# Expert rows transposed in 32x32 blocks by VectorE and moved through memory, expert weights resident in SBUF, a new order of steps

## What is computed

```python
x  = hidden                                  # (4, 512, 256) f32
xn = layernorm(x)
# attention part (RWKV): k, v, r are projections of xn mixed with xn one step earlier
m_new = max(mx + w, k); m_out = max(mx, k + time_first)
e1, e2 = exp(mx - m_out), exp(k + time_first - m_out)
out = (e1*num + e2*v) / (e1*den + e2)
e1, e2 = exp(mx + w - m_new), exp(k - m_new)
num, den = e1*num + e2*v, e1*den + e2        # scanned over 512 positions
s = (sigmoid(r) * out) @ Wo.T
# mixture of experts: 16 experts, each token takes 4
h = silu(xn @ w_gate[e]) * (xn @ w_up[e])    # 256 -> 256
ffn += coeff[:, None] * (h @ w_down[e])      # 256 -> 256
result = x + s * silu(ffn)
```

## Time and profile before

| what | value |
|---|---|
| median of 3 runs | 346.5 us (344.99 to 347.97) |
| the profiled execution | 347.63 us |
| its span, first to last instruction | 345.7 us |
| mean granted clock of TensorE | 0.965 |
| loop over units (39) | from about 83 us to 305 us |

### The profile page before, as it was taken

The page is one execution under the profiler, slowest core; times in us unless marked ns, Lnnn a source line. Parts: engine busy times, 40 slices in busy tenths (PEclk is TensorE's granted clock), DMA queues, the critical chain, the costliest instruction groups (busy, mean ns, idle before and its releaser), DMA issues.

```text
span 345.7 us, 4753 instructions
## 1 busy us (share of the span) xinstructions
PE 299.8 (87%) x1413; PEld 236.0 (68%) x1414; DVE 253.4 (73%) x498; ACT 153.3 (44%) x236; POOL 225.5 (65%) x223
## 2 busy tenths in 40 slices
PE   0798999797999999999999999999999999799000
PEld 0334444345888888888888888888888888588000
DVE  2879899859589597795995959959687010189992
ACT  1891864224644635628247273463652323172220
POOL 3500399948767777777777777777777724257363
PEclk9999999998999999999999999999999999999755
DMA  7894000043656557656475666656465698587132
GB/s 236 279 392 191 1 0 1 8 131 89 177 175 207 159 172 232 215 146 205 144 254 141 211 171 203 208 195 186 153 211 171 216 361 302 194 280 238 43 121 91
DMA packets 31723, 61.46 MB, mean 178 GB/s; under 512 B 4620, under 2 KB 22029, under 8 KB 31568
## 3 DMA queue, kind: packets, MB, share of 16 engines
q10 hardware_dynamic: 6848, 21.26, 19.8%
q1 hardware_dynamic: 17360, 21.24, 18.1%
q0 software_dynamic: 7488, 18.63, 17.3%
HBM read 48.52 MB, written 14.42 MB: 182 GB/s over the span
## 4 chain that ended last, share of the span: by engine, by line
PE 68%; DVE 12%; POOL 9%; DMA 6%; issue 3%; POOLq 0%; ACT 0%; ACTq 0%; DVEq 0%
PE ps L545 60%; POOL ohB L334 8%; DVE arena L983 5%; PE ps L650 5%; DMA rows<-y_rows 3%; PE ps L555 2%; DMA wrou<-wrouT_in 1%; DVE arena L998 1%; POOL arena L352 1%; DMA arena<-xn_rows,tok_idx 1%; DVE arena L758 1%; DVE rows L733 1%; DMA y_rows<-arena,e_idx 1%; DVE vT L767 1%; DVE rows L814 0%
## 5 line engine op out<-in xcount | busy, mean ns | idle before, releaser
L545 PE MATMUL ps<-arena,rows 128*128 128x256 f32 x624 | 142.8, 383 | 2.4 <-issue 2.4
L545 PEld LDWEIGHTS ps<-arena,rows 128*128 128x128 f32 x624 | 116.8, 192 | 17.2 <-issue 3.0
L352 POOL DMA_INDIRECT arena<-xn_rows,tok_idx x78 | 83.5, 1070 | 27.6 <-issue 21.0
L359 POOL DMA_INDIRECT y_rows<-arena,dst_idx x66 | 72.8, 1103 | 22.3 <-issue 19.8
L911 DVE TENSOR_TENSOR arena<-arena,ps 128x512 f32<-128x512 f32 x39 | 26.3, 675 | 65.7 <-PE ps L545 34.1
L545 PE MATMUL ps<-wdn,arena 128*128 x312 | 73.7, 380 | 0.0
L545 PEld LDWEIGHTS ps<-wdn,arena 128*128 128x128 f32 x312 | 59.3, 190 | 8.2 <-issue 0.3
L498 ACT COPY arena<-ps 128x512 f32<-128x512 f32 x39 | 22.8, 584 | 83.4 <-PE ps L545 83.4
L334 POOL TENSOR_SCALAR ohB<-late 128x128 f16<-128x128 f32 x24 | 30.7, 1291 | 24.9 <-DVE late L819 24.9
L545 PE MATMUL ps<-arena 128*128 128x512 f32 x96 | 45.5, 607 | 0.4 <-DVE arena L758 0.4
L493 ACT ACTIVATE arena<-ps 128x512 f32<-128x512 f32 x39 | 23.5, 602 | 27.5 <-PE ps L545 27.3
(11 more groups left out here) (140 smaller groups left out, 332.3 us busy)
## 6 DMA issues: line engine op xcount, KB each, us to landing
rows<-wgu_in ACTq DMA_DIRECT2D x39, 512.0 KB, 3.8
rows<-y_rows SPq DMA_DIRECT2D x3, 2048.0 KB, 11.1
wdn<-wd_in SPq DMA_DIRECT2D x1, 4096.0 KB, 14.4
rT<-x_in SPq DMA_DIRECT2D x4, 512.0 KB, 6.0
xn_rows<-rT SPq DMA_DIRECT2D x4, 512.0 KB, 3.6
kT<-x_in SPq DMA_DIRECT2D x8, 256.0 KB, 3.3
rows<-y_rows SPq DMA_DIRECT2D x8, 256.0 KB, 5.0
out<-arena SPq DMA_DIRECT2D x8, 256.0 KB, 2.1
```

What stands on the lines that cost most here:

```text
L352: pool.indirect_dma_start(out=xg[i % XG][:, j, :], out_offset=None, in_=xn_rows, in_offset=bass.IndirectOffsetOnAxis(ap=tok_idx[:, 2 * i + ...
L359: pool.indirect_dma_start(out=y_rows, in_=ysb[:, par, j, :], in_offset=None, out_offset=bass.IndirectOffsetOnAxis(ap=idx[:, n + j:n + j + ...
L545: ins = nc.tensor.matmul(dst, lhsT(c), rhs(c), start=(c == 0), stop=(c == C - 1))
```

## The change

Six things change together.

1. From unit 4 on (`EARLY`) PE no longer transposes x. DVE transposes the gathered rows in blocks of 32x32 (`quad_x`, one instruction on 128x512), three units ahead of `hidden` (`AHEAD`). SP stores the result to DRAM (256 KB, `store_x`) and loads it back with four DMAs of 64 KB that move the blocks to their partitions (`load_xT`). Units 0 to 3 are transposed by PE as before.
2. The gate and up weights of all 16 experts (8 MB) are loaded into SBUF once, in place of 512 KB for each unit. For each unit ACT copies its expert's weights (128x1024) to one of two small buffers (`copy_expert`).
3. PE's step is now `down(i - 2)` and then `gate_up(i)`.
4. DVE's parts 1 and 2 of the scan write two differences where they wrote four and a maximum (3 instructions fewer in a piece). ACT makes the four tensors from them with two Relu instructions (scale 1 and -1) ahead of the exp.
5. LAG goes from 6 to 8, and `gather(i)` waits for `quad_x(i - 4)`.
6. SP's stream now holds the stores and loads of x for every unit, and the loads of slots 0 to 2 of `y_rows` stand behind them all. The down weights are loaded in two halves.

The core of the diff:

```diff
-            def load_expert(i):
+            def copy_expert(i):
                 wait(act, up_psum, i - 1)
                 expert = act.value_load(unit_expert[0:1, i:i + 1], min_val=0, max_val=E - 1)
-                act.dma_start(wgu[:, i % 2].rearrange("p c n -> p (c n)"),
-                              wgu_in[bass.ds(expert, 1)].rearrange("a p n -> p (a n)")).then_inc(wgu_loaded[i % 2], 16)
+                nc.scalar.copy(wgu[i % 2].rearrange("p c n -> p (c n)"),
+                               wgu_all[:, bass.ds(expert, 1), :].rearrange("p a n -> p (a n)")).then_inc(wgu_copied, 1)
...
-            def step(i, blocks=None):
-                evac_x(i)
-                if i > 0:
-                    if i <= NEED and (i - 1) % HALF == 1:
-                        piece = (i - 1) // HALF
-                        act.wait_ge(args_ready, piece + 1)
-                        nc.scalar.activation(args, args, ACT.Exp).then_inc(exps_ready, 1)
-                    silu(i - 1, (i - 1) % 2)
-                    if i + 1 < NP:
-                        next_expert(i + 1, blocks)
+            def step(i):
+                if i < EARLY:
+                    evac_x(i)
                 if i > 1:
                     evac_y(i - 2, i % 2, 32 * ((i - 2) // 2))
+                if i < NEED and i % HALF == 1:
+                    act.wait_ge(args_ready, i // HALF + 1)
+                    for part, sign in ((args[:, 2:4, :], -1.0), (args[:, 0:2, :], 1.0)):
+                        nc.scalar.activation(part, gaps, ACT.Relu, scale=sign).then_inc(act_step, 1)
+                    act.wait_ge(act_step, 2 * (i // HALF + 1))
+                    nc.scalar.activation(args, args, ACT.Exp, scale=-1.0).then_inc(exps_ready, 1)
+                silu(i, i % 2)
+                if i + 2 < NP:
+                    copy_expert(i + 2)
...
+            def store_x(i):
+                sp.wait_ge(xq_ready, i - EARLY + 1)
+                sp.dma_start(xq_rows[i], xq[:, i % 2, :]).then_inc(xq_stored[i % 2], 16)
+
+            def load_xT(i, par, stored):
+                sp.wait_ge(up_psum, i - 1)
+                sp.wait_ge(xq_stored[par], stored)
+                for q in range(NQ):
+                    sp.dma_start(xTg[q * QUAD:(q + 1) * QUAD, par, :].rearrange("p (i n) -> p i n", i=NQ),
+                                 xq_rows[bass.ds(i, 1), :, q * P:(q + 1) * P].rearrange("a (i p) n -> p (a i) n", p=QUAD)
+                                 ).then_inc(xT_in[par], 16)
+
+            def step(i):
+                if i >= EARLY:
+                    store_x(i)
+                if i > EARLY:
+                    load_xT(i - 1, (i - 1) % 2, 16 * ((i - 1 - EARLY) // 2 + 1))
...
             def step(i):
-                transpose_x(i)
-                if i > 0:
-                    gate_up(i - 1, (i - 1) % 2, 16 * ((i - 1) // 2 + 1))
+                if i < EARLY:
+                    transpose_x(i)
...
                 if i > 1:
                     down(i - 2, i % 2, expert_of(i - 2))
+                gate_up(i, i % 2)
...
-                    V.scalar_tensor_tensor(out=e_keep, in0=m_old, scalar=w, in1=m_new, op0=ALU.add, op1=ALU.subtract)
-                    V.tensor_tensor(e_new, k, m_new, ALU.subtract)
-                    link(V.scalar_tensor_tensor(out=ta, in0=k, scalar=first, in1=m_old, op0=ALU.add, op1=ALU.max))
+                    V.scalar_tensor_tensor(out=gaps[:, 0], in0=m_old, scalar=w, in1=k, op0=ALU.add, op1=ALU.subtract)
                 elif part == 2:
-                    V.tensor_tensor(o_keep, m_old, ta, ALU.subtract)
-                    V.scalar_tensor_tensor(out=o_new, in0=k, scalar=first, in1=ta, op0=ALU.add,
+                    V.scalar_tensor_tensor(out=gaps[:, 1], in0=k, scalar=first, in1=m_old, op0=ALU.add,
                                            op1=ALU.subtract).then_inc(args_ready, 1)
...
+            def quad_x(i):
+                dve.wait_ge(xg_in[i % XG], 32 * (i // XG + 1))
+                if i >= EARLY + 2:
+                    dve.wait_ge(xq_stored[i % 2], 16 * ((i - EARLY) // 2))
+                V.transpose(xq[:, i % 2, :].rearrange("p (q m c) -> p m q c", q=NQ, c=QUAD),
+                            xg[i % XG].rearrange("p t (c q r) -> p (t c) q r", c=C, q=NQ)).then_inc(xq_ready, 1)
...
             def step(i):
+                next_quad_x(i + AHEAD)
                 piece, u = divmod(i, HALF)
```

More of the change, by code:

```diff
@@ L920, in wkv @@
                 m_old, m_new = mrun[:, 0:SEQ], mrun[:, 1:SEQ + 1]
[L921 removed]
+                e_new, o_keep, e_keep, o_new = (args[:, a, :] for a in range(4))
                 H = SEQ // 2
@@ L970, in step @@
                     wkv(piece // C, piece % C, part)
-            for i in range(FIRST - 1):
+            for i in range(FIRST):
+                if i == FIRST - AHEAD:
+                    blocks, low = units_used(dve)
                 step(i)
-            blocks, low = units_used(dve)
-            optional(dve, blocks, lambda i: step(i - 1))
-            hidden(low + LAG - 1, (FIRST - 1) % 2)
+            optional(dve, blocks, step)
             def weighted(n, k):
```

141 lines of the change are left out of this document (85 added, 56 removed).

## The result

| what | before | changed |
|---|---|---|
| median | 347.24 us (4 runs, 344.99 to 348.06) | 379.62 us (4 runs, 377.16 to 380.02) |
| ratio, 95% interval | 1 | 1.0944 (1.0899 to 1.0988) |
| the profiled execution, its span | 347.63, 345.7 us | 379.92, 378.2 us |
| mean granted clock | 0.965 | 0.936 |

The changed kernel is 9.4% slower, 13.6 us above the forecast of 366 and inside its range.

The account below looks back on a forecast made before the run. DVE with ACT was to become the bound in place of PE: 22.30 - 1.99 + 1.83 + 3.28 = 25.4 us a piece. With start, last units and tail the span is 365, + 1.93 - 1.13 gives 366 us; range 356 to 382.

Parts of the forecast that it names:

- transposes at the scan's price: Rival: each block transpose on DVE takes 1.22 us in place of 0.61, + 15 us: 381; chance 0.20 together with x late.
- units 29 to 38: End of the loop, PE alone setting the pace at last: last hidden at about 319 us, where it was 302.10, +17.
- What bounds the kernel: In the loop: PE needs 22.48 us a piece of four units; DVE with ACT, a closed loop, runs at 22.30.
- Transposes on DVE: In a piece: four block transposes at 0.61 us, one falling into DVE's wait, three lengthening the loop by 1.83 us.
- ACT in a piece: From args to hidden: two Relus and the exp's exposed table load add 3.28 us, between 2.0 and 3.5.
- The loop: DVE and ACT become the bound: 25.4 us a piece against PE's 20.7; seven such distances make 178 us, where it was 156.1.
- The start: First units: ACT's copies of experts' weights put hidden(1) at 98.4 in place of 95.85 us, +2.6, between 0 and +4.
- SP and the tail: After the loop: loads of slots 0 to 2 go out behind load_xT(38), at about 311 us, in a row; span 365.
- PE sets the pace: Rival: DVE and ACT need under 20.7 us a piece, all 15.4 us are kept: 334 us; faster had chance 0.04.
- x comes too late: Rival: in the last units PE waits for load_xT, 0.6 to some 5 us a unit: 374, up to 400.
- Transposes dearer or x late: The two rivals of dearer DVE transposes and late x taken together: 372 to 390 us, chance 0.20.
- The clock fell: Rival: PE's clock falls in its new pauses; 4 us at the lower level cost 2 us a piece, sum unchanged; chance 0.03.

Follow-up runs that it names:

- e4: Kernel before with only the two Relus on ACT in place of three DVE instructions: 357.59 us, ratio 1.0289.
- e5: Kernel before with one block transpose of 128x512 on DVE in each of 33 steps, of other data into an unread scratch: 360.22 us, ratio 1.0388.
- e1: Changed kernel with an exp of one column ahead of ACT's wait for the args, to load the exp's table there: 373.73 us, ratio 1.0697.
- e6: Changed kernel with all x transposed by PE, LAG 6, no block transposes and no stores and loads of x: 390.02 us, ratio 1.1225.
- e9: e8 with x of units 1 to 3 transposed by PE and copied by ACT one step earlier: 347.24 us, ratio 1.0041.
- e7: Changed kernel with SP's eight reads of counts ahead of the last load of x instead of behind it: 376.99 us, ratio 1.0874.
- e8: Changed kernel with silu of unit 4k + 1 ahead of the args' wait, exp's table loaded in that wait, SP's reads hoisted: 359.6 us, ratio 1.0333.
- e12: e9 with the load of slot 0 of y_rows ahead of the last load of transposed x: 349.21 us, ratio 1.0058.

## Why the prediction was right, and where its sizes were off

The direction, the mechanism and the range held; the time was 13.6 us low. That it still lies inside the range is in part luck: the upper end, 382, was set by transposes at the scan's price, and they did not cost that. What filled the room was the first piece, units 29 to 38 and the tail, for which the range had no term of this size. Step by step:

**What bounds the kernel.** "It takes 0.18 us less than PE needs, and that is all the room it has" carried the forecast, and it is shown: e4 and e5 each touch only the ring of DVE and ACT, and each shows up in full. In e5 not a single instruction was taken from or given to PE.

**Transposes on DVE.** 0.61 us each was forecast for a step; 0.63 were measured (duration 0.709), and one of the four was free. The rival at the scan's price of 1.22 falls. The estimate of 1.24 us that I had drawn from the Trainium skill, "VectorE: DVE Perf Modes", section "The three transpose paths", falls with it: scaling the page's bf16 figure by four for 512 columns of f32 gave 1.7 times the measured 0.709.

**ACT in a piece.** +3.28 forecast. e4 gives 1.31 + 1.99 = 3.30, and e1 that 1.27 of it is the table load. The drain behind each switch in the Trainium skill, "ScalarE: Activation LUTs", section "What ACT_TABLE_LOAD costs", does not show here: the exp starts 1.29 us after its load does (173.64 to 174.93) and the silu 1.30 us after (176.86 to 178.16).

**The loop.** 25.4 forecast, 25.46 measured, DVE's idle time "about 6.5" and 6.58. PE's pause was there, but 2.7 to 3.7 us in place of 4 to 5: its work in between took longer than the 20.7 us counted. A window over one piece of the changed kernel, with a mean granted clock of 0.93:

```profile
179.00:204.46 25.46, 22.76 (x96) 19.25 (x96) 18.57 (x27) 14.96 (x18) 17.42 (x16) 0.93 0.55 167
```

In the piece before it (153.32 to 178.79) the clock was 1.00 and PE was busy for 21.78 us, so the clock is only half of the difference; what the other half is stays open.

**The start.** `hidden(1)` 98.4 forecast, 98.32 measured. What failed is the assumption behind "seven distances between the `hidden` of units 1 and 29": the first is no ordinary piece. It took 29.5 us (98.32 to 127.82), +4.1. The forecast asked what the new order does to PE's products and not to units 0 to 3, whose x PE transposes in the step in which it needs it; e6 shows the price of that for each unit, and e9 the 12.6 us that come back when x is made one step ahead.

**Units 29 to 38.** 42.6 us forecast from `hidden(29)` to the last, 46.1 measured (280.64 to 326.75). The gain of the change does show here, where PE alone sets the pace: the kernel before took 50.1 (251.96 to 302.10). But DVE stands 1.74 us before the transpose at 284.93, where it reads the values of the run-time condition, three steps earlier than before. And the load of x of unit 34 stands on SP behind the store of unit 35, whose transpose comes late among DVE's parts. The chain of the changed kernel goes that way:

```profile
296.99 0.72 DVE late L1009
297.73 0.36 SPq L286
...
299.59 2.59 DMA arena<-xq_rows
302.22 15.82 PE ps L584 x72
```

From `hidden(34)` on it is 5.18 us a unit, as forecast; that is the time of the 24 products in the kernel before too, so the moving operand in runs of 32 columns costs nothing.

**SP and the tail.** 46 us forecast from the last `hidden` to the end, 51.45 measured. The wait of slot 0 behind load_xT(38) was right. The term that was too small is "slots 0 to 2 then go out in a row": it left out SP's eight reads of counts between load_xT(38) and slot 0, 4.7 us (318.35 to 323.02; e7, which moves them, ends 2.1 us sooner). The transfers were the smaller part: the forecast has the slots land 8, 6 and 8 us one after another, and they took 9.5, 7.0 and 7.5. DVE waited 5.14 and 4.15 us for the first two. From the landing of slot 2 on it was 31 us, where the forecast had 32.

The sum of the misses in the spans: -0.1 (start) + 4.1 (first piece) + 0.2 (six pieces) + 3.5 (units 29 to 38) + 5.5 (tail) = 13.2, for 378.2 - 365.

**The other rivals.** "PE sets the pace" was ruled out. It did not come with the ring opened either: a piece took 22.2 us in e8 and 21.7 at best in e9, not 20.7, with GpSimd at work without a pause. "x comes too late" was a small term in the changed kernel (PE waited for it 5.5 us in 6 places) and decided only in e12. "Transposes dearer or x late" had 0.20 for 372 to 390, where the time came to lie, but for neither of these reasons. The clock fell after one pause and not after another, as the forecast had it from the earlier trace rows. Windows of the changed kernel:

```profile
124.00:126.00 2.00, 0.99 (x5) 0.54 (x3) 0.00 (x0) 1.98 (x2) 1.39 (x3) 1.00 0.24 66
126.00:128.00 2.00, 0.00 (x0) 0.00 (x0) 0.18 (x1) 1.99 (x3) 1.62 (x2) 1.00 0.41 131
128.00:130.00 2.00, 1.35 (x3) 1.17 (x4) 1.97 (x3) 2.00 (x4) 1.46 (x2) 0.66 0.28 88
130.00:132.00 2.00, 2.00 (x6) 1.56 (x5) 1.97 (x3) 0.64 (x1) 1.70 (x2) 0.50 0.23 51
...
152.00:154.00 2.00, 0.00 (x0) 0.00 (x0) 0.68 (x2) 1.99 (x3) 0.82 (x1) 1.00 0.96 317
154.00:156.00 2.00, 1.86 (x9) 1.66 (x10) 1.93 (x4) 2.00 (x4) 1.02 (x1) 1.00 0.54 189
```

After a pause of some 3.7 us (what PE's rows leave of 124 to 130) the granted clock was 0.50 (1.2 GHz) at 130 to 132; after the next pause, some 2.9 us, it was 1.00 (2.4 GHz) at 154 to 156. By the Trainium skill, "TensorE: Matmul & The Clock Gate", Part 1, the clock is set back by an idle stretch that is long enough; these two pauses agree with that. Those of the earlier trace rows are in the other order: PE was idle for 1.88 us ahead of 82.06 and the clock fell, and for 2.35 us ahead of 298.09 and it did not. So the length of a pause alone does not tell. For the time it did not matter: pieces with a mean granted clock of 1.00 and of 0.93 took 25.47 and 25.46 us, so the lost time lay in PE's slack.

Of the 9.4%, e4 and e5 account for 2.9 and 3.9 points; the 2.7 that are left (about 9 us) are the later start, the first piece, the reads of the run-time condition and the tail, less the 4 us that PE gained in units 29 to 38. That split of the rest is read from the traces; only the start (e9) and SP's reads of counts (e7) were tried by themselves, and LAG 8 was not.

## What to carry to other kernels

An engine's idle time inside a ring of engines that wait for each other is part of the ring's length: before moving work off the busiest engine, add up the ring that runs next to it, and see on which side of its waits the new work falls. The same instruction costs nothing in front of a wait and its full time behind it (one table load, 1.27 us a piece), as long as the engine does wait there (in the first two pieces of e1 it did not). A stage order that hides a producer's latency has to be kept for the few first units that still use that producer. And long loads that move behind the loop meet its last short and urgent transfers, so the chain of each load, what must land before it may go out, belongs in the forecast.

## What the runs showed of the hardware that was not expected

- A transpose of 128x512 f32 in 32x32 blocks takes VectorE 0.709 us, 0.63 us in a row of instructions: the price of an ordinary operation of that shape.
- The Relu needs no table load of its own: it runs behind the silu's (L546 in the changed kernel) and behind the exp's (L548 in e1), so only the place of the exp's load was a cost.
- Eight values read into registers by SP took 4.7 us, as much as half a load of 2 MB.
- In the tail VectorE is held up by GpSimd's adds: in e12 one SCALAR_TENSOR_TENSOR of 128x256 took 8.23 us and ended when GpSimd had finished six adds of 128x512 of 1.26 to 1.28 us each (315.04 to 322.43); the median of that instruction is 0.48 us. In the kernel before the longest took 7.79 us, in the changed kernel 1.50. The Trainium skill, "SBUF — State Buffer", section "Who interferes with whom", has the two engines exclude each other at a shared port; the rows agree in kind, and the hold here lasted over six instructions in a row.
